# Three causal heads in a bank of sums instead of two, in a four-layer transformer kernel on one Trainium2 core

## The chip, the cores and the metric

One core of one Trainium2 chip runs the whole program in one launch. The metric is device time in microseconds (us) for one execution. The kernel before took 1213.9 us as the median of 3 runs (1211.96 to 1216.73).

## The reference

Two sequences of 1024 tokens, width 128, pass through four residual layers, each followed by a layer norm: causal attention with 16 heads of 8, a mixture of 8 experts (top 2 of 8, ReLU), a second causal attention with 16 heads of 8 whose queries and keys are low-rank products, and a last layer that is an attention without a mask (16 heads, 4 values a head) followed by a mixture of 8 experts with GELU. What this case touches is the end of each head's attention:

```python
attn = softmax(where(causal, scale * q @ k.T, -inf))   # per head, 1024 x 1024
ans  = attn @ v                                        # per head, 1024 x 8
x    = layernorm(x + ans_of_all_heads @ Wo.T + bo)
```

All arithmetic that the reference does in float32 is kept to float32 accuracy: queries and keys are split into three bf16 parts, and the product with the values is a float32 matmul.

## The kernel before

Engines run five instruction streams that are written out by hand and meet only at semaphores. There are 96 heads in all, numbered g: 0 to 31 are the first causal attention (16 heads for each of two sequences), 32 to 63 the second, 64 to 95 the attention without a mask. Run 0 is heads 0 to 31, then come 32 units of the first experts; run 1 is heads 32 to 95, then the second experts.

A causal head has 9 chunks of 512 columns in two batches (k=0 has five, k=1 four). For each chunk TensorE (PE) computes a block of scores by query (L1246), whose row maxima VectorE (DVE) takes two heads ahead (L974, L980), and a block of scores by key (L1261), which ScalarE (ACT) turns into probabilities (L864). Three banks (S1, S2) stand between PE and each of its two readers. `probs_by_v` then multiplies the probabilities of a batch by the values: 18 matmuls a head, in the order: batch 1 of the head before in this head's k=0, batch 0 of this head in its k=1. The maxima come back to PE through GpSimd (POOL, `split_max`, L673 to L680), one transpose on PE (`max_rows`, L1269), ACT (`rows`, L841) and a DMA.

The product with the values leaves its sums, transposed, in one bank, SUM. Its left operand is a head's tile of 32 columns in `v_heads`: POOL (`take_v`, L656) copies the head's 9 columns (a one for the denominator and 8 values) to the place of the head in its group and the other columns stay zero. So several heads can add into SUM side by side: a group. A causal group is two heads (2 x 9 = 18 of 32 columns), a group without mask four heads. There are four such value tiles, by g modulo 4.

When a group has ended, SUM has to be emptied:

- ACT `take_sums` (L846) copies the bank, PE waits for that before the first product of the next group
- PE `turn_sums` (L1296) turns it with 4 float32 transposes into the bank SHARED, at k=1 of the next head
- ACT `take_out` (L848) copies the used columns to `by_quarter`
- POOL `add_quarters` (L683) adds up the four quarters with 3 instructions, before its second mask and `split_max` of the same head
- DVE `normalise` (L990) takes a reciprocal and multiplies, in the middle of the head after that.

SHARED is used by nearly everything else too: `max_rows` of each head, and the steps of the surrounding layers (output projections, layer norms' transposes, routing, the next layer's queries, keys and values), which a table puts between the batches of given heads (L259 to L299). Each user of SHARED waits until the one before has been read out (`move_in`). The table's steps stand at the same heads before and after; the steps `aT` (turning the attention's output) wait for all groups of a sequence.

Of the kernel before, what the change touches and what calls it, by code (L numbers as in the profile page):

```python
# [1 line left out]

# [39 lines left out]
class Attention:  # L42


    def __init__(self, layer, head_dim, scale_dim, causal):
# [4 lines left out]
        self.dv = head_dim + 1  # L50
        self.group = 16 // head_dim
        self.scale = float(scale_dim) ** -0.5
# [39 lines left out]
class Head:  # L92


    def __init__(self, g):
# [4 lines left out]
        self.slot = g % RING  # L100
        self.first_of_group = self.n % self.a.group == 0
        self.ends_group = self.n % self.a.group == self.a.group - 1

# [28 lines left out]
GROUP = [sum(hd.ends_group for hd in HEADS[:g]) for g in range(3 * NH + 1)]  # L132
GROUPS = [[hd for hd in HEADS if GROUP[hd.g] == i] for i in range(GROUP[-1])]
ADDS = [sum(heads[0].a.adds for heads in GROUPS[:i]) for i in range(len(GROUPS) + 1)]

# [182 lines left out]
def build(nc, inp, out):  # L318
    ctx = ExitStack()
    with ctx:  # L320
        def sb(name, shape, dt=F32):
            return ctx.enter_context(nc.sbuf_tensor(name, shape, dt))
# [19 lines left out]
        v_all = [sb("v8", [P, NH, TB, 9]), sb("v4", [P, NH, TB, 5])]  # L342
        v_heads = [sb("v_head8", [P, RING, TB, Q]), sb("v_head4", [P, RING, TB, Q])]
        probs = sb("probs", [P, 9, CH])
        sums = sb("sums", [P, 2, CH])
        by_quarter = sb("by_quarter", [P, 2, 4, 4, 20])
        pairs = sb("pairs", [P, 4, 18])
        total = sb("total", [P, 2, TB, 20])
        tile_max = sb("tile_max", [P, RING, TB, 3])
# [45 lines left out]
        def v_head_of(a):  # L395
            return v_heads[0 if a.hd == 8 else 1]
# [179 lines left out]
        def _(pool):  # L576
# [79 lines left out]
            def take_v(g):  # L656
                hd = HEADS[g]
                a = hd.a
                ge(pool, "pv", BATCHES[max(g - RING + 1, 0)])
                if a.layer == 0 and hd.n == 0:  # L660
                    pool.wait_ge(sem("v_first"), NCH)
                if a.layer > 0 and hd.h == 0:
                    taken(pool, "v", a.layer, BY_SEQUENCE[hd.b][-1])
                at = a.dv * (hd.n % a.group)
                nc.gpsimd.tensor_copy(v_head_of(a)[:, hd.slot, :, at:at + a.dv], v_of(a)[:, hd.n, :, :]
                                      ).then_inc(sem("v_head"), 1)
# [16 lines left out]
            def add_quarters(i):  # L683

                a = GROUPS[i][0].a
                q = by_quarter[:, i % 2, :, :, 0:a.group * a.dv]
                pool.wait_ge(sem("by_quarter"), i + 1)
                ge(pool, "normalised", 2 * (i - 1))
                if not a.causal:
                    nc.gpsimd.tensor_tensor(  # L690
                        total[:, i % 2, :, 0:a.group * a.dv].rearrange("p (half t) d -> p t half d", half=2),
                        q[:, :, 0:4:2, :], q[:, :, 1:4:2, :], ALU.add).then_inc(sem("total"), 1)
                    return
                ge(pool, "total", ADDS[i])
                nc.gpsimd.tensor_tensor(pairs[:], q[:, :, 0, :], q[:, :, 1, :], ALU.add).then_inc(sem("total"), 1)  # L695
                pool.wait_ge(sem("total"), ADDS[i] + 1)
                nc.gpsimd.tensor_tensor(total[:, i % 2, 4:8, 0:18], pairs[:], q[:, :, 2, :], ALU.add
                                        ).then_inc(sem("total"), 1)
                nc.gpsimd.tensor_copy(total[:, i % 2, 0:4, 0:18], q[:, :, 3, :]).then_inc(sem("total"), 1)

# [41 lines left out]
        def _(act):  # L742
# [105 lines left out]
            def take_out(i):  # L848
                a = GROUPS[i][0].a
                act.wait_ge(sem("out"), i + 1)  # L850
                ge(act, "total", ADDS[max(i - 1, 0)])
                nc.scalar.activation(by_quarter[:, i % 2, :, :, 0:a.group * a.dv],  # L852
                                     SHARED[:].rearrange("p (t g c) -> p t g c", t=4, g=4)[:, :, :, 0:a.group * a.dv],
                                     ACT.Copy).then_inc(sem("by_quarter"), 1)
# [54 lines left out]
        def _(dve):  # L909
# [80 lines left out]
            def normalise(i):  # L990
                first = GROUPS[i][0]
                a, G, h = first.a, first.a.group, first.h
                o = total[:, i % 2, :, 0:G * a.dv].rearrange("p t (g d) -> p t g d", g=G)
# [177 lines left out]
        def _(pe):  # L1171
# [100 lines left out]
            def probs_by_v(g, k):  # L1272
# [10 lines left out]
                for c, b in a.pv_order[k]:  # L1283
                    if c in a.masked and (c, b) == next(y for y in a.pv_order[k] if y[0] == c):
# [4 lines left out]
                    this = (c, b, half, quarter)  # L1289
                    ins = mm(SUM[Q * quarter:Q * (quarter + 1), q:q + P * count], v_head_of(a)[:, hd.slot, j, :],  # L1290
                             probs[:, hd.probs_place(c), at:at + P * count],
# [11 lines left out]
            def between(place):  # L1303
                for step in BETWEEN[place]:
# [3 lines left out]
                    if kind == "aT":  # L1308
                        L, c = which
                        a = ATTENTIONS[L]  # L1310
                        groups_done = (L * NH + H * (c // CB + 1)) // a.group if L < 2 else (
                            GROUP[2 * NH] + H * (c // CB + 1) // a.group)
                        pe.wait_ge(sem("normalised"), 2 * groups_done)
# [208 lines left out]
```

## Time and profile before

| | |
|---|---|
| median of 3 runs | 1213.9 us |
| the profiled execution | 1214.44 us, of which its span 1212.7 us, granted PE clock 0.985 |
| PE busy | 1108.5 us (91%) |
| DVE busy | 870.5 us (72%) |
| ACT busy | 777.6 us (64%) |
| POOL busy | 270.3 us (22%) |

Busy time says which engine works, and not which one the others wait for. In the causal heads the program is periodic, so the time between two equal instructions of neighbouring heads says directly what a head costs. The instruction used for that is `rows` (L841 on ACT), once a head, at the end of its first batch.

### The profile page before, as it was taken

What the parts mean: (1) busy time and instruction counts of PE and PEld (TensorE: products, weight loads), DVE (VectorE), ACT (ScalarE), POOL (GpSimd) and SP (SyncE); (2) the same over time, 40 slices, a digit from 0 to 9 for tenths busy, and PEclk for the clock granted to TensorE, in tenths of its full rate; (3) what the DMA queues carried; (4) which work ended last, traced back from release to release, by engine and by line L of the source; (5) the groups of instructions that cost most, each with busy time, mean ns of one, the idle gap of its engine ahead of it and who ended that gap; (6) DMA issues with size and microseconds to landing.
All of it is one profiled execution on the core that took longest, in us unless ns stands there. A gap on an engine that the chain in (4) does not pass through costs nothing. (4 is left out here: it accounts for less than half of the span.)

```text
span 1212.7 us, 24956 instructions
## 1 busy us (share of the span) xinstructions
PE 1108.5 (91%) x8799; PEld 605.9 (50%) x8872; DVE 870.5 (72%) x2077; ACT 777.6 (64%) x1563; POOL 270.3 (22%) x819
## 2 busy tenths in 40 slices
PE   8899998999999988999988998888888898899996
PEld 6466665656766655666655642221112221137774
DVE  4888887773434377888766899899999889904433
ACT  4376766667444436777666667888888778874443
POOL 4244332332002013533233421111110011000001
PEclk9899999999999999999999999999999989999999
DMA  7245431110001701243211321102111000000000
GB/s 192 57 111 135 113 93 32 40 32 2 1 1 23 165 11 41 74 104 95 71 48 58 62 39 33 29 12 35 37 33 29 20 12 16 7 1 1 10 9 18
DMA packets 39550, 57.67 MB, mean 48 GB/s; under 512 B 9393, under 2 KB 14977, under 8 KB 39041
## 3 DMA queue, kind: packets, MB, share of 16 engines
q1 hardware_dynamic: 39424, 56.06, 18.7%
q8 instruction: 71, 1.16, 0.4%
q14 instruction: 55, 0.44, 0.1%
HBM read 30.81 MB, written 24.64 MB: 46 GB/s over the span
## 5 line engine op out<-in xcount | busy, mean ns | idle before, releaser
L864 ACT ACTIVATE probs<-bank 128x512 f32<-128x512 f32 x1088 | 574.6, 601 | 235.2 <-PE bank L1261 234.2
L980 DVE TENSOR_REDUCE tile_max<-bank 128x1 f32<-128x512 f32 (+3 forms) x1152 | 612.3, 593 | 38.0 <-PE bank L1246 33.3
L1246 PE MATMUL bank<-qk 125*128 125x128 bf16 (+2 forms) x1664 | 389.0, 312 | 59.1 <-DVE tile_max L980 46.7
L1261 PE MATMUL bank<-qk 128*128 128x128 bf16 (+4 forms) x1607 | 362.8, 306 | 5.7 <-ACT probs L864 5.3
L1290 PE MATMUL bank<-probs,v_head 128*32 128x512 f32 (+3 forms) x3328 | 304.3, 454 | 0.1
L1246 PEld LDWEIGHTS bank<-qk 125*128 125x128 bf16 (+1 forms) x1664 | 132.2, 97 | 316.9 <-DVE tile_max L980 244.2
L1147 DVE SCALAR_TENSOR_TENSOR acc<-bank,gate,acc 128x128 f32<-128x128 f32 x256 | 72.0, 344 | 156.7 <-PE bank L1417 156.7
L1290 PEld LDWEIGHTS bank<-probs,v_head 128*32 128x32 f32 x3328 | 139.7, 109 | 52.8 <-issue 29.8
L1261 PEld LDWEIGHTS bank<-qk 128*128 128x128 bf16 (+1 forms) x1664 | 133.2, 97 | 56.8 <-ACT probs L864 21.0
L884 ACT ACTIVATE probs<-bank,sb_b 128x512 f32<-128x512 f32 x128 | 81.0, 684 | 117.9 <-PE bank L1406 117.9
L974 DVE TENSOR_REDUCE tile_max<-bank 128x4 f32<-128x512 f32 x128 | 87.4, 688 | 87.0 <-PE bank L1246 86.7
L1417 PEld LDWEIGHTS bank<-sb_w,probs 128*128 128x128 f32 x1024 | 123.1, 192 | 24.5 <-issue 24.0
L1417 PE MATMUL bank<-sb_w,probs 128*128 128x128 f32 x1024 | 124.7, 275 | 0.0
L1406 PE MATMUL bank<-xT,sb_w 128*128 128x512 f32 x256 | 121.0, 595 | 0.0
L705 POOL TENSOR_SCALAR_AFFINE_SELECT probs<-probs 128x512 f32<-128x512 f32 x128 | 81.6, 638 | 133.6 <-ACT probs L864 133.4
L673 POOL CAST neg_parts<-neg_max 128x8 bf16<-128x8 f32 x96 | 18.5, 193 | 325.9 <-DVE neg_max L987 325.9
L1406 PEld LDWEIGHTS bank<-xT,sb_w 128*128 128x128 f32 x256 | 43.9, 191 | 34.1 <-issue 33.8
L695 POOL TENSOR_TENSOR pairs<-by_quarter 128x72 f32<-128x72 f32 x32 | 11.0, 344 | 159.3 <-ACT by_quarter L852 159.3
L1241 PE MATMUL bank<-mask,ident 128*128 128x512 bf16 x112 | 43.7, 391 | 2.6 <-DVE tile_max L980 1.2
L841 ACT ACTIVATE neg_rows<-bank 24x128 bf16<-24x128 bf16 x96 | 24.7, 257 | 20.2 <-PE bank L1269 20.2
L641 POOL TENSOR_SCALAR rstd<-mean_var 128x4 f32<-128x4 f32 (+1 forms) x12 | 2.9, 238 | 146.0 <-DVE mean_var L1038 145.7
L804 ACT ACTIVATE x<-x_plus,shift,rstd 128x128 f32<-128x128 f32 x64 | 26.2, 487 | 9.8 <-POOL shift L644 9.8
(133 smaller groups left out, 659.8 us busy)
## 6 DMA issues: line engine op xcount, KB each, us to landing
qk<-qk_parts SPq DMA_DIRECT2D x160, 144.0 KB
qk_parts<-q_parts SPq DMA_DIRECT2D x48, 192.0 KB, 2.4
qk_parts<-k_parts SPq DMA_DIRECT2D x48, 192.0 KB, 3.0
qk_parts<-q_parts SPq DMA_DIRECT2D x24, 96.0 KB, 2.3
qk_parts<-k_parts SPq DMA_DIRECT2D x24, 96.0 KB, 2.9
sb_w<-in_w SPq DMA_DIRECT2D x8, 256.0 KB, 3.8
sb_w<-in_w SPq DMA_DIRECT2D x2, 1024.0 KB, 5.6
qk<-neg_rows SPq DMA_DIRECT2D x96, 6.0 KB
```

The costliest lines, as they stand in the source:

```text
L705: nc.gpsimd.affine_select(out=p, in_=p, compare_op=ALU.is_ge, fill=0.0, base=0, pattern=[[0, 4], [1, P]], channel_multiplier=-1).then_inc( ...
L864: nc.scalar.activation(probs[:, hd.probs_place(c), :], S2[i % len(S2)][:], ACT.Exp, scale=hd.a.scale).then_inc(sem("probs"), 1)
L884: nc.scalar.activation(hidden[:, m % 2, fb, :], bank[2 * (m % 2) + fb][:], ACT.Relu if f == 0 else ACT.Gelu, bias=w_sb[f"b1_{f}"][:, FB * ...
L974: ins = nc.vector.tensor_reduce(tile_max[:, hd.slot, 4 * c:4 * c + 4, 0], s1[:].rearrange("p (t k) -> p t k", k=P), AX.X, ALU.max)
L980: ins = nc.vector.tensor_reduce(tile_max[:, hd.slot, t, which:which + 1], s1[:, at:at + P * count], AX.X, ALU.max)
L1147: ins = nc.vector.scalar_tensor_tensor(acc[:, tile, :], Y[m % 2][:, P * t:P * (t + 1)], gate[:, tile, e:e + 1], acc[:, tile, :], ALU.mult, ...
L1241: mm(s1[:], ident16[:], mask16[:].rearrange("p t k -> p (t k)"), start=True, stop=False, skip_group_check=True)
L1246: ins = mm(s1[:, at:at + P * count], qk[hd.query_rows, hd.place, 0, P * t:P * (t + 1)], qk[hd.query_rows, hd.place, 1, P * k0:P * (k0 + co ...
L1261: ins = mm(s2[:, at:at + P * count], qk[hd.key_rows, hd.place, 1, P * j:P * (j + 1)], qk[hd.key_rows, hd.place, 0, P * q0:P * (q0 + count) ...
L1290: ins = mm(SUM[Q * quarter:Q * (quarter + 1), q:q + P * count], v_head_of(a)[:, hd.slot, j, :], probs[:, hd.probs_place(c), at:at + P * co ...
L1406: ins = mm(bank[2 * (m % 2) + fb][:], w_sb[f"w1_{f}"][:, e, P * fb:P * (fb + 1)], xT[:, tokens(c)], start=True, stop=True)
L1417: ins = mm(Y[m % 2][:, P * t:P * (t + 1)], hidden[:, m % 2, fb, P * t:P * (t + 1)], w_sb[f"w2_{f}"][:, e, fb, :], start=fb == 0, stop=fb = ...
```

## The change

The 16 causal heads of a sequence are grouped 3, 3, 3, 3, 2, 2 where they were grouped in eight pairs. A group of three uses 27 of the 32 columns. Because a value tile's zero columns must stay zero, a tile now belongs to a place in the group: six tiles, three places for each of two alternating groups, and `take_v` waits for the head that used the same tile last. The evacuation of a group, its three adds and its normalisation work on 27 columns a tile where the group has three heads, and on 18 where it has two. The attention without a mask keeps its groups of four.

```diff
-        self.group = 16 // head_dim
+        self.groups = (3, 3, 3, 3, 2, 2) if causal else (4, 4, 4, 4)
...
-        self.first_of_group = self.n % self.a.group == 0
-        self.ends_group = self.n % self.a.group == self.a.group - 1
+        ends = list(accumulate(self.a.groups))
+        group = sum(self.h >= end for end in ends)
+        self.at_in_group = self.h - ends[group] + self.a.groups[group]
+        self.first_of_group = self.at_in_group == 0
+        self.ends_group = self.h == ends[group] - 1
+        self.v_slot = self.at_in_group + 3 * (group % 2) if self.a.causal else self.slot
...
+V_BEFORE = {hd.g: max((o.g for o in HEADS[:hd.g] if o.a.causal == hd.a.causal and o.v_slot == hd.v_slot), default=None)
+            for hd in HEADS}
...
-        v_heads = [sb("v_head8", [P, RING, TB, Q]), sb("v_head4", [P, RING, TB, Q])]
+        v_heads = [sb("v_head8", [P, 6, TB, Q]), sb("v_head4", [P, RING, TB, Q])]
-        by_quarter = sb("by_quarter", [P, 2, 4, 4, 20])
-        pairs = sb("pairs", [P, 4, 18])
-        total = sb("total", [P, 2, TB, 20])
+        by_quarter = sb("by_quarter", [P, 2, 4, 4, 27])
+        pairs = sb("pairs", [P, 4, 27])
+        total = sb("total", [P, 2, TB, 27])
...
-                ge(pool, "pv", BATCHES[max(g - RING + 1, 0)])
+                if V_BEFORE[g] is not None:
+                    pool.wait_ge(sem("pv"), BATCHES[V_BEFORE[g] + 1])
...
-                at = a.dv * (hd.n % a.group)
-                nc.gpsimd.tensor_copy(v_head_of(a)[:, hd.slot, :, at:at + a.dv], v_of(a)[:, hd.n, :, :]
+                at = a.dv * hd.at_in_group
+                nc.gpsimd.tensor_copy(v_head_of(a)[:, hd.v_slot, :, at:at + a.dv], v_of(a)[:, hd.n, :, :]
...
-                nc.gpsimd.tensor_tensor(pairs[:], q[:, :, 0, :], q[:, :, 1, :], ALU.add).then_inc(sem("total"), 1)
+                nc.gpsimd.tensor_tensor(pairs[:, :, 0:wide], q[:, :, 0, :], q[:, :, 1, :], ALU.add).then_inc(sem("total"), 1)
...
-                a = GROUPS[i][0].a
+                wide = GROUPS[i][0].a.dv * len(GROUPS[i])
...
-                a, G, h = first.a, first.a.group, first.h
+                a, G, h = first.a, len(GROUPS[i]), first.h
...
-                        groups_done = (L * NH + H * (c // CB + 1)) // a.group if L < 2 else (
-                            GROUP[2 * NH] + H * (c // CB + 1) // a.group)
+                        groups_done = GROUP[L * NH + H * (c // CB + 1)]
```

How the streams change is seen at two places. The first is PE in head 34, the third of the second causal attention, from the last scores of its batch 1 to the product with the values and the projection behind it. Before (L1261 scores by key, L1300 the turn of the sums, L1290 the product with the values, L1369 a projection of the table):

```order
L1261 MATMUL bank<-qk 128x384 [waits probs]
L1261 MATMUL bank<-qk 128x128
L1300 MATMUL bank<-ident,sums 128x128 [waits taken,sums]
L1300 MATMUL bank<-ident,sums 128x128 x3
L1290 MATMUL bank<-probs,v_head 32x512 [waits probs,sums,v_head]
L1290 MATMUL bank<-probs,v_head 32x512 x2
L1290 MATMUL bank<-probs,v_head 32x256
L1290 MATMUL bank<-probs,v_head 32x128 [waits masked]
L1290 MATMUL bank<-probs,v_head 32x256
L1290 MATMUL bank<-probs,v_head 32x128 x3
L1369 MATMUL bank<-xT,wk_eff 128x512 [waits by_quarter,taken,loaded_attn1]
```

The same place in the changed kernel (its lines are 10 or 11 higher):

```order
L1272 MATMUL bank<-qk 128x384 [waits probs]
L1272 MATMUL bank<-qk 128x128
L1301 MATMUL bank<-probs,v_head 32x512 [waits probs,v_head]
L1301 MATMUL bank<-probs,v_head 32x512 x2
L1301 MATMUL bank<-probs,v_head 32x256
L1301 MATMUL bank<-probs,v_head 32x128 [waits masked]
L1301 MATMUL bank<-probs,v_head 32x256
L1301 MATMUL bank<-probs,v_head 32x128 x3
L1379 MATMUL bank<-xT,wk_eff 128x512 [waits taken,loaded_attn1]
```

The turn of the sums, with its wait for SHARED (`taken`) and for `sums`, has left head 34; it stands in head 35 now.

The second place is POOL in head 52, from the copy of a value tile (L665) to the splitting of the next maxima (L673). Before:

```order
L665 COPY v_head<-v 128x8x9 [waits pv]
L695 TENSOR_TENSOR pairs<-by_quarter 128x72 [waits total,normalised,by_quarter]
L697 TENSOR_TENSOR total<-pairs,by_quarter 128x4x18 [waits total]
L699 COPY total<-by_quarter 128x4x18
L705 AFFINE_SELECT probs<-probs 128x512 [waits probs]
L641 TENSOR_SCALAR rstd<-mean_var 128x8 [waits var]
L642 TENSOR_TENSOR rstd<-rstd,minus_half 128x8 [waits gpsimd_chain]
L643 TENSOR_TENSOR shift<-mean_var,rstd 128x8 [waits gpsimd_chain]
L644 TENSOR_SCALAR shift<-shift 128x8 [waits gpsimd_chain]
L673 CAST neg_parts<-neg_max 128x8 [waits neg_max,neg_ps]
```

In the changed kernel:

```order
L675 COPY v_head<-v 128x8x9 [waits pv]
L716 AFFINE_SELECT probs<-probs 128x512 [waits probs]
L650 TENSOR_SCALAR rstd<-mean_var 128x8 [waits var]
L651 TENSOR_TENSOR rstd<-rstd,minus_half 128x8 [waits gpsimd_chain]
L652 TENSOR_TENSOR shift<-mean_var,rstd 128x8 [waits gpsimd_chain]
L653 TENSOR_SCALAR shift<-shift 128x8 [waits gpsimd_chain]
L683 CAST neg_parts<-neg_max 128x8 [waits neg_max,neg_ps]
```

The three adds of the sums, which wait for ACT's `by_quarter`, are gone from between the copy and the mask; they stand in head 51, as 128x108.

## Rows read from the trace of the kernel before

**Rows 1.** Timeline of ACT: start us, duration us, engine, line, operation (heads 1 to 4).
```profile
54.95 0.26 ACT L841 ACTIVATE neg_rows<-bank 24x128 bf16<-24x128 bf16 x1
...
62.03 0.26 ACT L841 ACTIVATE neg_rows<-bank 24x128 bf16<-24x128 bf16 x1
...
69.56 0.26 ACT L841 ACTIVATE neg_rows<-bank 24x128 bf16<-24x128 bf16 x1
...
76.86 0.26 ACT L841 ACTIVATE neg_rows<-bank 24x128 bf16<-24x128 bf16 x1
```
**Rows 2.** Timeline of PE in head 40, the turn and what follows.
```profile
519.62 0.60 PE L1300 MATMUL bank<-ident,sums 128*128 128x128 f32 x4
520.15 1.51 PE L1290 MATMUL bank<-probs,v_head 128*32 128x512 f32 x18
```
**Rows 3.** Timeline of DVE (the multiply of `normalise`, heads 41 and 5) and POOL (head 5).
```profile
525.00 0.29 DVE L997 TENSOR_TENSOR a_tok<-total,den_inv 128x128 f32<-128x128 f32 x1
...
84.51 0.48 DVE L997 TENSOR_TENSOR a_tok<-total,den_inv 128x128 f32<-128x128 f32 x1
...
83.55 1.29 POOL L631 TENSOR_TENSOR x_plus<-x,sb_bo 128x512 f32<-128x512 f32 x1
```
**Rows 4.** Groups by shape: busy us, mean ns of one.
```profile
L995 DVE RECIPROCAL den_inv<-total 128x16 f32<-128x16 f32 x32 | 7.8, 245 | 7.3 <-POOL total L699 7.3
...
L995 DVE RECIPROCAL den_inv<-total 128x32 f32<-128x32 f32 x8 | 2.7, 344 | 0.0
...
L1027 DVE TENSOR_TENSOR x_plus<-x,acc 128x512 f32<-128x512 f32 x4 | 2.9, 718 | 0.0
...
L695 POOL TENSOR_TENSOR pairs<-by_quarter 128x72 f32<-128x72 f32 x32 | 11.0, 344 | 159.3 <-ACT by_quarter L852 159.3
...
L690 POOL TENSOR_TENSOR total<-by_quarter 128x160 f32<-128x160 f32 x8 | 4.2, 522 | 56.1 <-ACT by_quarter L852 56.1
...
L852 ACT ACTIVATE by_quarter<-bank 128x288 f32<-128x288 f32 x32 | 13.5, 422 | 1.3 <-PE bank L1300 1.2
```
**Rows 5.** Timeline of POOL, end of `split_max`, and of PE, its reader, head 41.
```profile
523.09 0.20 POOL L680 TENSOR_TENSOR neg_parts<-neg_rest,neg_parts 128x8 bf16<-128x8 f32 x1
...
524.14 0.23 PE L1269 MATMUL bank<-ident,neg_parts 128*24 128x128 bf16 x1
```
**Rows 6.** Timeline of PE, turns in heads 34, 56 and 18.
```profile
472.20 0.63 PE L1300 MATMUL bank<-ident,sums 128*128 128x128 f32 x4 [0.94 <-DVE rest L937]
...
659.75 0.63 PE L1300 MATMUL bank<-ident,sums 128*128 128x128 f32 x4 [1.06 <-DVE rest L938]
...
185.68 0.63 PE L1300 MATMUL bank<-ident,sums 128*128 128x128 f32 x4 [0.22 <-ACT aT L794]
```
**Rows 7.** Timeline of ACT, heads 52 and 21.
```profile
612.33 0.25 ACT L841 ACTIVATE neg_rows<-bank 24x128 bf16<-24x128 bf16 x1
...
623.20 0.25 ACT L841 ACTIVATE neg_rows<-bank 24x128 bf16<-24x128 bf16 x1
...
210.13 0.26 ACT L841 ACTIVATE neg_rows<-bank 24x128 bf16<-24x128 bf16 x1
...
218.96 0.25 ACT L841 ACTIVATE neg_rows<-bank 24x128 bf16<-24x128 bf16 x1
```
**Rows 8.** Timeline of PE around the start of head 53.
```profile
621.33 0.23 PE L1269 MATMUL bank<-ident,neg_parts 128*24 128x128 bf16 x1 [2.01 <-POOL neg_parts L680]
...
623.59 1.08 PE L1338 MATMUL bank<-ident,x 128*128 128x128 f32 x4 [1.17 <-ACT neg_rows L841]
```
**Rows 9.** Busy time by stretch; the third number from the end is the granted PE clock.
```profile
622.00:625.00 3.00, 1.83 (x17) 1.25 (x11) 0.00 (x0) 1.45 (x4) 0.07 (x1) 0.67 0.01 2
625.00:628.00 3.00, 2.78 (x26) 1.77 (x27) 2.67 (x6) 2.18 (x5) 0.83 (x2) 0.76 0.05 8
```
**Rows 10.** Timeline of POOL at the start of the program.
```profile
7.59 1.90 POOL L608 MEMSET v_head<- 128x1024 f32 x2
...
14.43 2.28 POOL L618 TENSOR_TENSOR k_parts<-rest,k_parts 128x512 bf16<-128x512 f32 x2 [4.57 <-ACT k_parts L754]
```

More of the change, by code:

```diff
@@ L1 @@
 from contextlib import ExitStack
+from itertools import accumulate
 import concourse.bass as bass
@@ L685, in add_quarters @@
                 a = GROUPS[i][0].a
-                q = by_quarter[:, i % 2, :, :, 0:a.group * a.dv]
+                wide = a.dv * len(GROUPS[i])
+                q = by_quarter[:, i % 2, :, :, 0:wide]
                 pool.wait_ge(sem("by_quarter"), i + 1)
@@ L690, in add_quarters @@
                     nc.gpsimd.tensor_tensor(
-                        total[:, i % 2, :, 0:a.group * a.dv].rearrange("p (half t) d -> p t half d", half=2),
+                        total[:, i % 2, :, 0:wide].rearrange("p (half t) d -> p t half d", half=2),
                         q[:, :, 0:4:2, :], q[:, :, 1:4:2, :], ALU.add).then_inc(sem("total"), 1)
@@ L694, in add_quarters @@
                 ge(pool, "total", ADDS[i])
-                nc.gpsimd.tensor_tensor(pairs[:], q[:, :, 0, :], q[:, :, 1, :], ALU.add).then_inc(sem("total"), 1)
+                nc.gpsimd.tensor_tensor(pairs[:, :, 0:wide], q[:, :, 0, :], q[:, :, 1, :], ALU.add).then_inc(sem("total"), 1)
                 pool.wait_ge(sem("total"), ADDS[i] + 1)
-                nc.gpsimd.tensor_tensor(total[:, i % 2, 4:8, 0:18], pairs[:], q[:, :, 2, :], ALU.add
+                nc.gpsimd.tensor_tensor(total[:, i % 2, 4:8, 0:wide], pairs[:, :, 0:wide], q[:, :, 2, :], ALU.add
                                         ).then_inc(sem("total"), 1)
-                nc.gpsimd.tensor_copy(total[:, i % 2, 0:4, 0:18], q[:, :, 3, :]).then_inc(sem("total"), 1)
+                nc.gpsimd.tensor_copy(total[:, i % 2, 0:4, 0:wide], q[:, :, 3, :]).then_inc(sem("total"), 1)
             def mask(g, which):
@@ L848, in take_out @@
             def take_out(i):
-                a = GROUPS[i][0].a
+                wide = GROUPS[i][0].a.dv * len(GROUPS[i])
                 act.wait_ge(sem("out"), i + 1)
                 ge(act, "total", ADDS[max(i - 1, 0)])
-                nc.scalar.activation(by_quarter[:, i % 2, :, :, 0:a.group * a.dv],
-                                     SHARED[:].rearrange("p (t g c) -> p t g c", t=4, g=4)[:, :, :, 0:a.group * a.dv],
+                nc.scalar.activation(by_quarter[:, i % 2, :, :, 0:wide],
+                                     SHARED[:].rearrange("p (t g c) -> p t g c", t=4, g=4)[:, :, :, 0:wide],
                                      ACT.Copy).then_inc(sem("by_quarter"), 1)
@@ L1289, in probs_by_v @@
                     this = (c, b, half, quarter)
-                    ins = mm(SUM[Q * quarter:Q * (quarter + 1), q:q + P * count], v_head_of(a)[:, hd.slot, j, :],
+                    ins = mm(SUM[Q * quarter:Q * (quarter + 1), q:q + P * count], v_head_of(a)[:, hd.v_slot, j, :],
                              probs[:, hd.probs_place(c), at:at + P * count],
```

## The prediction

> **What bounds the kernel now.** I read the timeline of ACT first, for the time from one `rows` to the next in the causal heads. A head is one of three kinds. In a turn head the group of the head before is evacuated (PE's four transposes); in a normalise head, the one after it, DVE does the two instructions of `normalise`; in a plain head neither happens. The kernel before has turn and normalise heads in strict alternation, with one plain head in the clear, head 1, before any group has ended. Plain 62.03 - 54.95 = 7.08 us, turn 69.56 - 62.03 = 7.53, normalise 76.86 - 69.56 = 7.30 [rows 1]. The same 7.53 and 7.30 come back in the quiet heads of both layers. So a group boundary costs 0.45 + 0.22 us over two plain heads, whatever the engines' busy shares say.
>
> Next the timeline of PE says what the 0.45 is: PE has no idle in a turn head, and from the turn's first transpose to the product behind it is 520.15 - 519.62 = 0.53 us [rows 2]. PE ends that head. In the normalise head DVE's work in the middle makes PE wait for a bank of maxima. How directly it does so is seen where POOL works beside it: in head 5 a 1.29 us POOL addition of a bias started at 83.55, and the multiply at 84.51 took 0.48 instead of 0.29 [rows 3]; that head's period is longer by about the same 0.19. Time added to `normalise` comes through one for one.
>
> Last come the heads in which a turn meets a step of the table, since the change moves turns: PE's own waits before L1300 [rows 6] and the costliest wait at a max transpose [rows 8].
>
> **The change part by part.**
>
> Groups. A sequence had 8 turn and 8 normalise heads; with turns behind heads 2, 5, 8, 11, 13 and 15 it has 6 turn, 6 normalise and 4 plain heads. Over four sequences 8 turns go at 0.45 = -3.6 us and 8 normalisations at 0.22 = -1.8 us [rows 1]. ACT's and POOL's share of a boundary (copying the bank, evacuating 288 columns at 0.42, the adds) lies beside PE's work and is counted as nothing. What is late next in a plain head is what is late in head 1: PE's own matmuls and DVE's maxima, both near 7.0.
>
> Biases. The four POOL bias additions of layer 0 run in heads 5, 7, 9, 11, and one of layer 1 in head 37, all normalise heads before. Of these only head 7 is one afterwards. 4 x 0.19 = -0.8 us [rows 3]. Bounds: 0 (they disturb something else) to -0.9. The Trainium skill, "SBUF — State Buffer", in its terms on the shared port pair, says that VectorE and GpSimd hold it exclusively for a whole instruction and the loser is fully blocked. By that rule each multiply would wait for the end of the bias addition, 84.84 - 84.51 = 0.33, and the sum would be 0.6 lower; the row shows 0.19, so the trace agrees only in direction.
>
> Wider work. 16 groups have 27 columns a tile where 18 were. On DVE: the reciprocal goes from 16 to 24 elements, halfway between 245 and 344 ns, +0.05; the multiply gets 64 more elements, at (718 - 292)/384 = 1.1 ns (292 is the 128-element multiply, 0.29 in the rows) +0.07 [rows 3, 4]. 16 x 0.12 = +1.9 us, all exposed as argued. Bounds: 0, and in proportion to the columns, half of 0.245 + 0.29, so 16 x 0.27 = +4.3. I take 1.9, as it has a slope from rows. On ACT and POOL: the evacuation 0.42 becomes at most 0.63; the two-input adds cost (522 - 344)/88 = 2.0 ns an element, so 344 becomes 417 [rows 4], the three together +0.2. `split_max` is queued behind them on POOL, and PE's max transpose waits for it: `split_max` ends 523.29, the transpose starts 524.14, so 0.85 us are free [rows 5]. Even in proportion (+0.46 for the adds, +0.21 on ACT) it fits. Cost nothing.
>
> Value tiles. `take_v` waits for a product that is 4 to 6 heads old, or older, instead of 4: never later than before. The value tile's clearing at the start grows from 1024 to 1536 elements, half of 1.90/2 = +0.5 us on POOL (at most +0.95), which then waits 4.57 us for ACT anyway [rows 10]. Nothing.
>
> Turns that leave a collision. Before, PE in heads 34 and 56 reached the turn while SHARED still held queries of the next layer, not yet read out: it waited 0.94 and 1.06 us [rows 6]. Both become plain heads. The product behind does not use SHARED, and the next user comes behind it, 1.5 us later [rows 2], so the wait goes: -2.0. Heads 18 and 50 waited 0.22 each for `aT` and become plain: -0.4 [rows 6]. In exchange turns come to heads 19, 25, 35, 51 and 57. Only in 35 (values of the next layer) and 51 (a projection) does SHARED have a tenant from the same head; both are read out by DVE at about the time PE arrives. Bounds 0 to 2 x 1.06; I take +0.3, an estimate: a readout by one quick instruction, as the 0.22 us wait for `aT`, in each or less. Together -2.1 us.
>
> Head 52. Here POOL had the three adds, the mask and the root of the layer norm ahead of `split_max`, and PE stood 2.01 us at the max transpose, then 1.17 for SHARED [rows 8]. The period was 623.20 - 612.33 = 10.87. Head 21 has the same steps of the other layer in a normalise head, without adds: 218.96 - 210.13 = 8.83 [rows 7]. In the changed kernel head 52 is a normalise head. 10.87 - 8.83 = 2.04, of which 7.53 - 7.30 = 0.23 is already counted: -1.8 us. After these waits PE's granted clock was 0.67 and 0.76 over two stretches of 3 us, that is 1.2 GHz instead of 2.4 for 2 x 0.33 x 3 = 2.0 and 2 x 0.24 x 3 = 1.4 us [rows 9]. If PE no longer stands so long, the matmuls in 3.4 us run in half the time: up to -1.7; bounds 0 and -1.7, I take half, -0.9, since another wait for SHARED remains there.
>
> Sum: -3.6 - 1.8 - 0.8 + 1.9 - 2.1 - 1.8 - 0.9 = -9.1 us. Against the profiled execution's 1214.44 (span 1212.7 and 1.7 around it) that is 1205.3. The median of the runs is 0.5 lower than that execution, less than their spread, so I leave 1205.3. All else, experts and attention without mask, is taken as unchanged.
>
> **The rivals.**
>
> A. The collisions only move. The table is dense in heads 17 to 28 and 49 to 56, and a turn in 19, 25, 35 or 51 or a wider normalisation in 52 can meet what the old ones met. For it: three of the old turns waited on exactly such steps. Against: head 21 shows the combination of head 52 without harm. Then only the regular part is left: -3.6 - 1.8 - 0.8 + 1.9 = -4.3, so 1210.1.
>
> B. A plain head in the steady state is no better than a normalise head, because head 1 stands next to the start and nothing else shows the kind; DVE is then the next limit. Turns give 8 x 0.23 = -1.8, normalisations 0, the rest as summed (-0.8 + 1.9 - 2.1 - 1.8 - 0.9): -5.5, so 1208.9; with A too, 1213.7. Against: a turn head has no idle on PE, so without the turn 7.53 - 0.53 = 7.00 us of PE's work are left [rows 1, 2], which is near head 1.
>
> C. More comes off: the wider normalisation is hidden (0 instead of +1.9) and the whole 1.7 of clock comes back: -11.8, so 1202.6.
>
> D. Slower: POOL's chain from the evacuation over the wider adds to `split_max` gets so long that PE waits at the max transpose in each of the 16 wide turn heads, as it did in head 52. It bites from 0.85 us of growth [rows 5]. Growth of 1.4 eats the whole gain (16 x 0.57 = 9.1). At 1.9, adds some three times as long, 16 x 1.05 = 16.8, so 1205.3 + 16.8 = 1222.1. Against: the rows' slopes give 0.3 and proportion 0.67.
>
> **How the numbers follow.** Forecast 0.53, own range 1202.5 to 1208; A 0.20; B 0.12 (a third of it with A); C 0.09; D 0.06. What a measurement can tell from no change is about 0.5%, 6.1 us: faster means below 1207.8. Forecast 0.50 and C 0.09, little of B 0.04 and of A 0.03: faster 0.66. Same: most of A and B and a rest of the forecast, 0.28. D makes slower 0.06. The range 1200.5 to 1211.5 takes in C with some clock beyond it, A and most of B, and is open to D and to B with A.
>
> **What would show it.** In the quiet heads of each layer `rows` should come at 7.53, 7.42, 7.08 in turn; 7.3 for the third means B. `normalise` should be about 0.30 and 0.36 us long. PE should have no wait before the turn over 0.3 us, else A. The 2.01 us wait before the max transpose of head 53 should be gone, and the clock dip with it or halved. POOL's `pairs` addition should take 0.42 us; a growing count of PE waits for `neg_parts` means D. I am wrong if the experts or heads from 65 on change by more than a microsecond.

## The result, and the profile after

The changed kernel took 1208.9 us (median of 6 runs, 1207.54 to 1212.2) against 1213.5 for the kernel before on the same chip (6 runs, 1211.96 to 1216.73): ratio 0.9958, 95% interval 0.9945 to 0.9972, 4.6 us or 0.4% less. The forecast was 9.1 us less, and 1208.9 lies 0.9 above its own range (1202.5 to 1208), inside the wide one (1200.5 to 1211.5). The 0.4% is below the 0.5% from which on the prediction spoke of faster, so by this measurement its likeliest outcome did not come. A second measurement of the same kernel (first experiment) gave 0.9935 (0.992 to 0.9951), 7.3 less, with 17 runs of before beside it. The profiled execution of the first, 1212.2 us (span 1210.5, granted clock 0.982), is the slowest of its six. So the lines in this section are from its profile, but the sums by head further down are made from the second's, 1207.9 (span 1206.2, clock 0.986). From profile to profile the heads agree to 0.01 or 0.02 us, except where the clock fell.

PE is busy 1106.1 us (91%), DVE 868.8, ACT 772.7, POOL 268.1: each engine within 5 us of before, which doesn't say where the difference lies.

The first view is ACT's timeline in heads 1 to 4, which answers to [rows 1] (the lines are 11 higher).

```profile
55.92 0.26 ACT L852 ACTIVATE neg_rows<-bank 24x128 bf16<-24x128 bf16 x1
...
63.00 0.26 ACT L852 ACTIVATE neg_rows<-bank 24x128 bf16<-24x128 bf16 x1
...
70.09 0.26 ACT L852 ACTIVATE neg_rows<-bank 24x128 bf16<-24x128 bf16 x1
...
77.62 0.26 ACT L852 ACTIVATE neg_rows<-bank 24x128 bf16<-24x128 bf16 x1
```

Heads 1 and 2 are plain, 7.08 and 7.09, and head 3 is the turn, 7.53. The quiet heads repeat 7.53, 7.41, 7.08.

The wider operations, by shape (busy us, mean ns of one), beside [rows 3, 4]:

```profile
L1008 DVE TENSOR_TENSOR a_tok<-total,den_inv 128x192 f32<-128x192 f32 x16 | 6.8, 425 | 0.5
L706 POOL TENSOR_TENSOR pairs<-by_quarter 128x108 f32<-128x108 f32 x16 | 6.7, 419 | 80.1 <-ACT by_quarter L863 80.1
L1006 DVE RECIPROCAL den_inv<-total 128x24 f32<-128x24 f32 x16 | 4.7, 292 | 0.0
```

The reciprocal's 292 (forecast 295) and the add's 419 (417) are as read from the slopes, and ACT's evacuation takes 0.535 us (at most 0.63 was allowed for). The multiply's mean, 425, is above the 0.36 us that it takes alone: two of the 16 are long. They belong to what was missed. This is DVE and POOL in head 36 and then in head 7:

```profile
487.56 1.01 DVE L1008 TENSOR_TENSOR a_tok<-total,den_inv 128x192 f32<-128x192 f32 x1
...
487.19 1.16 POOL L627 TENSOR_TENSOR q_parts<-rest,q_parts 128x512 bf16<-128x512 f32 x1
...
99.80 0.79 DVE L1008 TENSOR_TENSOR a_tok<-total,den_inv 128x192 f32<-128x192 f32 x1
...
99.09 1.28 POOL L640 TENSOR_TENSOR x_plus<-x,sb_bo 128x512 f32<-128x512 f32 x1
```

And in head 57, now a turn head, PE waits for POOL. The timelines of PE and POOL there:

```profile
662.86 0.61 PE L1311 MATMUL bank<-ident,sums 128*128 128x128 f32 x4
...
669.29 0.23 PE L1280 MATMUL bank<-ident,neg_parts 128*24 128x128 bf16 x1 [1.84 <-POOL neg_parts L690]
```

```profile
664.17 0.42 POOL L706 TENSOR_TENSOR pairs<-by_quarter 128x108 f32<-128x108 f32 x1 [5.00 <-ACT by_quarter L863]
...
665.23 0.64 POOL L716 TENSOR_SCALAR_AFFINE_SELECT probs<-probs 128x512 f32<-128x512 f32 x1
665.83 1.15 POOL L627 TENSOR_TENSOR q_parts<-rest,q_parts 64x512 bf16<-64x512 f32 x1
666.95 1.15 POOL L627 TENSOR_TENSOR k_parts<-rest,k_parts 64x512 bf16<-64x512 f32 x1
668.05 0.18 POOL L683 CAST neg_parts<-neg_max 128x8 bf16<-128x8 f32 x1
...
669.04 0.20 POOL L690 TENSOR_TENSOR neg_parts<-neg_rest,neg_parts 128x8 bf16<-128x8 f32 x1
```

The turn itself waits for nothing. But behind the three adds (the first is shown) and the mask POOL has two instructions of a step of the table. They split off the third bf16 part of queries and keys for the layer without mask (the "thirds" from here on), 2.3 us together, and `split_max` comes behind them. The last two of these four rows of ACT show what it costs: 8.96 us for head 57 (660.59 to 669.55), where the normalise head before took 7.30.

```profile
611.15 0.25 ACT L852 ACTIVATE neg_rows<-bank 24x128 bf16<-24x128 bf16 x1
620.24 0.25 ACT L852 ACTIVATE neg_rows<-bank 24x128 bf16<-24x128 bf16 x1
...
660.59 0.25 ACT L852 ACTIVATE neg_rows<-bank 24x128 bf16<-24x128 bf16 x1
669.55 0.27 ACT L852 ACTIVATE neg_rows<-bank 24x128 bf16<-24x128 bf16 x1 [1.28 <-PE bank L1280]
```

The first two rows are head 52: 9.09, where [rows 7] gave 10.87. PE's max transpose at its end waits for nothing (it waited 2.01 [rows 8]); the wait for SHARED behind it is still there, 1.59 us where it was 1.17:

```profile
620.63 0.63 PE L1348 MATMUL bank<-ident,x 128*128 128x128 f32 x4 [1.59 <-ACT neg_rows L852]
```

After it PE's clock is at full in the stretches of [rows 9]:

```profile
622.00:625.00 3.00, 2.80 (x34) 2.18 (x33) 1.23 (x4) 2.67 (x7) 0.79 (x4) 1.00 0.31 98
625.00:628.00 3.00, 2.91 (x32) 1.65 (x29) 3.00 (x7) 2.89 (x7) 0.83 (x2) 1.00 0.00 0
```

### The profile page after: what moved, and what is told of

It reads as the page before. It is cut to its first block and busy times, and to the rows that moved or that the text cites. A ratio compares the mean times of both kernels' runs of the same rounds, so it can differ in the third digit from the quotient of the medians.

```text
span 1210.5 us, 24804 instructions
## 1 busy us (share of the span) xinstructions
PE 1106.1 (91%) x8768; PEld 605.3 (50%) x8840; DVE 868.8 (72%) x2061; ACT 772.7 (64%) x1547; POOL 268.1 (22%) x795
## 5 line engine op out<-in xcount | busy, mean ns | idle before, releaser
L706 POOL TENSOR_TENSOR pairs<-by_quarter 128x108 f32<-128x108 f32 (+1 forms) x24 | 9.5, 395 | 122.5 <-ACT by_quarter L863 122.5
```

## The experiments

Each edit is to the changed kernel, except where it says otherwise.

### The same kernel again, and groups of two in the new tiles

`a_again` has no edit. `two_by_place` keeps the tiles by place and everything else, with pairs in them:

```diff
-        self.groups = (3, 3, 3, 3, 2, 2) if causal else (4, 4, 4, 4)
+        self.groups = (2, 2, 2, 2, 2, 2, 2, 2) if causal else (4, 4, 4, 4)
```

> The changed kernel again, unaltered, to see which differences from the kernel before come back. Theory 1 (a fixed cost per kind of head plus meetings of turns with steps of the table): the same periods to 0.02 us in the quiet heads (7.53, 7.41, 7.08), 8.96 in head 57 and 8.06 in head 36, while the extra 1.6 us of head 23 and the 2.9 us of heads 61 to 63, where the granted PE clock fell, are not tied to the change and need not come back; ratio to before 0.9955 to 0.9965. Theory 2 (the moved turns bring the clock down at heads 23 and 61 to 63): both dips come back at the same heads with the same cost.

> One part of the change alone: six value tiles by place, evacuation and adds with a width by group, but groups of two heads everywhere. Theory 1 (all of the effect is in the number of groups): turn 7.53 and normalise 7.30 in every pair of heads, ratio to before 0.999 to 1.001. Rival (take_v's later wait or the larger clearing at the start counts): the start of head 0 moves by 0.5 us or more, ratio off by 0.002 or more.

Measured on one chip: 1207.9 us (0.9935) for the changed kernel again, and 1215.5 (12 runs) with pairs, ratio 1.0005 (0.9993 to 1.0017).

In `a_again` the quiet heads and heads 57 and 36 come back as expected. Of the falls of the clock, the one in head 23 came back (11.17) and those in heads 61 to 63 did not, so each theory was right about one of them.

With pairs the heads' periods add up to 0.24 us over before. Its first `rows` comes at 41.19 us, 0.9 later than before, which the rival asked for, but the changed kernel itself has it at 41.11 in one profile and 39.92 in the other, so a single start says nothing. The tiles, their larger clearing and `take_v`'s wait cost nothing that these runs can show; the gain is the grouping's.

### The steps that the new heads met, moved

The table counts in batches, half a head each. POOL's thirds for queries and keys come three batches after their step by default; `thirds_later` puts the last at five, one head later (58, a normalise head now). `all_moved` also moves the thirds of head 36 by half a head, and the bias addition of head 7 by one head.

```diff
-place = put_qkv(2, 1, later(place, 3))
+place = put_qkv(2, 1, later(place, 3), (0, 1, 2, 5))
```

```diff
-for c, g in enumerate((4, 6, 8, 10)):
+for c, g in enumerate((4, 7, 8, 10)):
...
-def put_next_qkv(c, place):
+def put_next_qkv(c, place, offsets=range(4)):
...
-    return put_qkv(1, c, later(place, 1))
+    return put_qkv(1, c, later(place, 1), offsets)
...
-put_next_qkv(3, at_head(32, 0))
+put_next_qkv(3, at_head(32, 0), (0, 1, 2, 4))
```

> The changed kernel with the step `third` of head 57 moved to head 58 (and the stores that follow it one head later). Theory 1 (in head 57 POOL has three wider adds, the mask and two thirds of 1.15 us ahead of split_max, and PE waits 1.84 us for it): head 57 falls from 8.96 to 7.53, the 1.84 us wait before the max transpose goes, head 58 stays within 0.3 of 7.57, in sum -1.3 to -1.7 us against the changed kernel. Rival (the wait only moves to head 58, or the time is given back in heads 61 to 63, where DVE is the bound): heads 57 to 64 together lose less than 0.4 us.

> The same, and two more moves of steps away from normalise heads: the bias addition of head 7 to head 8, the thirds of head 36 half a head later. Theory 1 (POOL's two-input instructions hold up the wide multiply of normalise on DVE: it took 1.01 us in head 36 instead of 0.36): head 36 falls from 8.06 to 7.45, head 7 from 7.84 to 7.41, in sum -2.3 to -2.8 us against the changed kernel, ratio to before 0.9935 to 0.9945. Rival (the long multiply is not on the path of PE): the multiply gets short and the periods stay.

`thirds_later` took 1205.5 us (1204.9 to 1207.6), 0.9921 (0.9907 to 0.9936), 2.4 below the unaltered kernel on the same chip. Its heads 57 and 58 together are 1.6 shorter, which the theory had at 1.3 to 1.7; the rest is not explained by the move. Heads 57 and 58 in ACT's timeline, and PE's max transpose in the former, which has no wait now:

```profile
658.91 0.25 ACT L852 ACTIVATE neg_rows<-bank 24x128 bf16<-24x128 bf16 x1
666.44 0.26 ACT L852 ACTIVATE neg_rows<-bank 24x128 bf16<-24x128 bf16 x1
673.86 0.26 ACT L852 ACTIVATE neg_rows<-bank 24x128 bf16<-24x128 bf16 x1
...
665.70 0.23 PE L1280 MATMUL bank<-ident,neg_parts 128*24 128x128 bf16 x1
```

7.53 and 7.42, the quiet values. So the 1.4 us that head 57 took over a quiet turn head is the meeting of the adds with the thirds in one POOL queue. In `all_moved` the multiply of head 36 is alone and takes 0.36:

```profile
487.14 0.36 DVE L1008 TENSOR_TENSOR a_tok<-total,den_inv 128x192 f32<-128x192 f32 x1
```

Head 36 takes 7.42 instead of 8.06, and head 7 7.42 instead of 7.84: the heads show the 1.1 us. The time does not: 1206.2 us, 0.9919 (0.9904 to 0.9934), no different from `thirds_later`, and 1.7 below the unaltered kernel where 2.3 to 2.8 was expected. In its profile the clock fell in head 23, as in the unaltered kernel.

### The same collision made in the kernel before

`before_thirds` is the kernel before with the last thirds moved from its head 57 (normalise there) to head 58 (a turn there), the edit of `thirds_later`.

> The kernel before, groups of two, with the thirds of head 57 moved to head 58, which is a turn head in it. Theory 1 (adds, mask and thirds in one turn head make POOL late for split_max): the mirror image of what happened in head 57 of the changed kernel, a wait of PE for POOL of 1.3 to 1.9 us in head 58 and a period of about 9 instead of 7.53, total +1.3 to +1.8 us, ratio 1.001 to 1.0015. Rival (the wait in head 57 came from the wider adds and not from the meeting): head 58 stays under 7.9.

ACT's and PE's timeline in that head:

```profile
673.99 0.26 ACT L841 ACTIVATE neg_rows<-bank 24x128 bf16<-24x128 bf16 x1
682.58 0.27 ACT L841 ACTIVATE neg_rows<-bank 24x128 bf16<-24x128 bf16 x1 [0.90 <-PE bank L1269]
...
682.31 0.23 PE L1269 MATMUL bank<-ident,neg_parts 128*24 128x128 bf16 x1 [1.46 <-POOL neg_parts L680]
```

8.59 us where it took 7.53, +1.1 (about 9 was expected), and PE waits 1.46 for the same tile; head 59 behind it takes 7.56 instead of 7.30. The mechanism belongs to a turn head whose adds and thirds both stand ahead of `split_max` in POOL's queue, whatever the width of the groups. It is the order that matters: in the kernel before, thirds also ran at head 36, a turn head, but they had ended 2.1 us before its adds, and the head took the quiet 7.53. That the wider adds deepen the wait fits its 1.84 us against 1.46, in two different heads. The whole time, 1216.5 us in 10 runs, 1.0009 (0.999 to 1.0028), is too coarse for it.

### Each part of a boundary doubled

`turn_twice` turns the sums twice, `multiply_twice` does the multiply of `normalise` once more beforehand into an unused tile, `pairs_twice` the first of POOL's adds.

```diff
-                for t in range(4):
+                for t in [0, 1, 2, 3] * 2:
```

```diff
+                nc.vector.tensor_tensor(
+                    spare[:, i % 2, :, 0:G * a.hd].rearrange("p t (g d) -> p t g d", g=G),
+                    o[:, :, :, 1:a.dv], den_inv[:, i % 2, :, 0:G].unsqueeze(3).to_broadcast([P, TB, G, a.hd]),
+                    ALU.mult)
```

```diff
+                nc.gpsimd.tensor_tensor(spare[:, i % 2, :, 0:wide], q[:, :, 0, :], q[:, :, 1, :], ALU.add)
```

> The changed kernel with the four transposes of each turn of the sums done twice into the same places (32 turns, 30 of them in heads). Theory (PE alone ends a turn head): each of the 22 causal turn heads gets longer by 0.53 us, 7.53 becomes 8.06, while the turn heads of the attention without mask, where DVE is busier, grow by less; in sum +11 to +17 us. Rival (the turn head is set by ACT or DVE and the transposes lie in a gap): under +5 us.

> The changed kernel with normalise's multiply done once more into an unused tile before the real one. Theory (DVE's time in normalise comes through to PE one for one): wide normalise heads go from 7.41 to about 7.7 and those of two heads from 7.29 to about 7.5. Rival (part is hidden): the quiet normalise heads grow by less than 0.15 us.

> The changed kernel with POOL's first add of the quarters done once more into an unused tile, +0.42 us ahead of split_max in each wide turn head. Theory (0.85 us were free in quiet turn heads, a little over 0.5 are left): quiet turn heads stay 7.53, head 57, where PE already waits for POOL, grows by 0.4. Rival D of the prediction (POOL's chain is at the edge): quiet turn heads grow by 0.2 us or more.

`turn_twice`, ACT around its turn head 3 and the doubled turn on PE:

```profile
68.32 0.26 ACT L852 ACTIVATE neg_rows<-bank 24x128 bf16<-24x128 bf16 x1
76.28 0.26 ACT L852 ACTIVATE neg_rows<-bank 24x128 bf16<-24x128 bf16 x1
...
70.59 1.04 PE L1311 MATMUL bank<-ident,sums 128*128 128x128 f32 x8
```

7.96 for 7.53: a second turn costs 0.43, as the first does (7.53 - 7.09 = 0.44). The theory had 0.53, the distance in [rows 2] from the first transpose to the product; 0.1 of it isn't added by the turn. The turn heads without mask grow by the same (head 72 from 11.03 to 11.47), not by less. There are 24 turns of causal groups and 8 of the others, 32 x 0.43 = 13.8; measured 1220.6 us, 1.0055 (1.0037 to 1.0073), that is 6.4 above before where the unaltered kernel is 7.3 below: 13.7. So close an agreement has luck in it: the medians are from two chips, and the two profiles' spans differ by 15.7, with falls of the clock in different heads.

`multiply_twice` (a single run, 1214.6 us), ACT around its wide normalise head 4:

```profile
76.80 0.27 ACT L853 ACTIVATE neg_rows<-bank 24x128 bf16<-24x128 bf16 x1
84.48 0.27 ACT L853 ACTIVATE neg_rows<-bank 24x128 bf16<-24x128 bf16 x1
```

7.68 for 7.41, +0.27 for an instruction whose row says 0.36. But 0.36 isn't what it takes from DVE. Here are the added multiply and the real one behind it, DVE in the same head:

```profile
76.97 0.36 DVE L1009 TENSOR_TENSOR spare<-total,den_inv 128x192 f32<-128x192 f32 x1
77.24 0.35 DVE L1013 TENSOR_TENSOR a_tok<-total,den_inv 128x192 f32<-128x192 f32 x1
```

They start 0.27 apart: the row's duration overlaps the next instruction by 0.09. With groups of two the starts are 0.20 apart, and those heads grow by 0.20 (7.29 to 7.49). So time added to `normalise` comes through one for one, as the theory and the prediction had it, if it is read from start to start. The forecast's 0.12 for the wider work holds too. From the start of the reciprocal to the next maximum DVE takes 0.60 us in a wide head and 0.49 in a narrow one, and the heads take 7.41 and 7.30. Of the 0.49 a narrow normalise head shows 0.21 over a plain one, so the first 0.28 is hidden, and what comes on top is not.

In head 36 the same edit costs 1.21 us, from 8.06 to 9.27. DVE and POOL there:

```profile
486.83 0.99 DVE L1009 TENSOR_TENSOR spare<-total,den_inv 128x192 f32<-128x192 f32 x1
487.75 1.30 DVE L1013 TENSOR_TENSOR a_tok<-total,den_inv 128x192 f32<-128x192 f32 x1
...
486.45 1.16 POOL L628 TENSOR_TENSOR q_parts<-rest,q_parts 128x512 bf16<-128x512 f32 x1
487.56 1.27 POOL L628 TENSOR_TENSOR k_parts<-rest,k_parts 128x512 bf16<-128x512 f32 x1
```

Each multiply runs into a POOL instruction of its own and ends 0.21 and 0.22 us after it (487.82 against 487.61, 489.05 against 488.83).

`pairs_twice` (a single run, 1212.3 us), ACT in the quiet turn head 41, then PE in head 57:

```profile
524.89 0.26 ACT L854 ACTIVATE neg_rows<-bank 24x128 bf16<-24x128 bf16 x1
532.42 0.26 ACT L854 ACTIVATE neg_rows<-bank 24x128 bf16<-24x128 bf16 x1
...
669.93 0.23 PE L1282 MATMUL bank<-ident,neg_parts 128*24 128x128 bf16 x1 [2.15 <-POOL neg_parts L691]
```

In a quiet turn head 0.4 more on POOL costs nothing (7.53). In head 57 the wait grows from 1.84 to 2.15, by 0.3 where 0.4 was expected. So the room that the prediction read from [rows 5] is there, and used up where POOL has a step. The delay shows in two normalise heads as well: in heads 7 and 36 POOL's long instruction starts later, the multiply beside it takes 1.13 and 1.37 us instead of 0.79 and 1.01, and the heads grow by the same 0.34 and 0.36.

### A head in which the clock fell

Head 23 took 9.57 us before and 11.17 after. It is a normalise head in both, and wider work can't be 1.6 us. In both, the step that turns `x` waits 2.01 us for SHARED, until ACT's `rows` has read the maxima out. Behind that wait the clock fell in the profile of after and not in that of before. The stretch that follows it, before and after, busy time and granted clock (third number from the end):

```profile
230.00:234.00 4.00, 4.00 (x42) 3.10 (x40) 2.22 (x6) 2.27 (x5) 1.42 (x5) 1.00 0.22 74
```

```profile
230.00:234.00 4.00, 4.00 (x35) 2.69 (x33) 1.27 (x3) 1.45 (x3) 0.79 (x4) 0.75 0.22 74
```

`xt_later` moves the step that waits (turning `x`) one head on, out of the way of that wait; `moved_xt` has it and the three other moves.

```diff
-put_routing(0, 0, put_attention_out(0, 0, at_head(17, 1), (0, 1, 2, 4, 5, 7, 8, 10, 11, 12)),
+put_routing(0, 0, put_attention_out(0, 0, at_head(17, 1), (0, 1, 2, 4, 5, 7, 8, 10, 12, 13)),
```

> The changed kernel with the second transposing step `xT` of the first attention moved from the middle of head 23 to its end, and the routing steps behind it half a head later. Theory 1 (in head 23 PE stands 2.01 us for SHARED because ACT does a layer norm before it reads out the maxima; the granted clock then falls or not depending on how that wait lies, 11.17 with the fall and 9.57 without): without the wait PE goes on, the clock stays at 2.4 GHz through head 23, and heads 22 to 29 together lose 2.5 to 4 us against the changed kernel. Theory 2 (the fall of the clock comes from the moved turn at head 22 or 25 and not from the wait): head 23 keeps a stretch with a granted clock of 0.5 to 0.7 and a period over 10.5.

> All moves together: thirds of head 57, bias of head 7, thirds of head 36 and the second xT of the first attention. Theory 1: the parts add up, ratio to before 0.988 to 0.991. Rival (the routing steps, half a head later, meet the turns of heads 25 and 28 or the end of the run and give it back): 0.9915 or more.

ACT's `rows` of `xt_later` in heads 22 to 24, and the moved transposes:

```profile
227.32 0.25 ACT L852 ACTIVATE neg_rows<-bank 24x128 bf16<-24x128 bf16 x1
234.17 0.27 ACT L852 ACTIVATE neg_rows<-bank 24x128 bf16<-24x128 bf16 x1
245.00 0.25 ACT L852 ACTIVATE neg_rows<-bank 24x128 bf16<-24x128 bf16 x1
...
229.93 0.66 PE L1348 MATMUL bank<-ident,x 128*128 128x128 f32 x4
...
243.85 0.39 PE L1257 MATMUL bank<-qk 125*128 125x256 bf16 x2 [1.83 <-DVE tile_max L991]
```

Its stretch behind the transposes:

```profile
230.00:234.00 4.00, 4.00 (x44) 2.71 (x43) 2.93 (x7) 2.71 (x6) 0.83 (x2) 1.00 0.17 62
```

The wait of 2.01 is gone, the clock stays at full, and head 23 takes 6.85. But head 24 takes 10.83 where it took 7.98, with 1.83 us of waiting for DVE's maxima: the work came along. Heads 22 to 29 together took 2.04 less than in the profile of after, where 2.5 to 4 was expected, and of that 1.6 is the clock fall that it had and this one had not. Nor does the full clock in head 23 tell the theories apart, since the kernels with the step in its old place have it in some profiles too (below). The time, 1208.5 us, 0.9943 (0.9925 to 0.9962), is that of the unaltered kernel. A miss. `moved_xt` took 1205.1 us, 0.9917 (0.9899 to 0.9934), again that of `thirds_later`: the parts did not add up in the time, and the rival's 0.9915 or more is what came.

Last, `all_moved` and `moved_xt` were measured again, as `all_moved_2` and `moved_xt_2`, since 6 runs each could not tell them apart.

> The version with the three moves of POOL steps again, beside the version with all four moves on the same chip. Theory 1: its heads 23 and 57 have 11.17 and 7.53 as before; it is 1 to 3 us slower than the version with all moves. Rival (what xT later saves is lost to the clock elsewhere): the two are within 0.5 us.

> The version with all four moves again. Theory 1: heads 23 and 24 have 6.85 and 10.83, the clock stays up in 23; 1 to 3 us faster than the version with three moves, ratio to before 0.990 to 0.992.

`all_moved_2` took 1205.6 us, 0.9924 (0.9901 to 0.9948), and `moved_xt_2` 1204.6, 0.9903 (0.9878 to 0.9929). Their intervals overlap, and they stay together. What they do settle is something about head 23. Here are PE's transposes in `all_moved` and the granted clock over the stretch behind them, and then both in `all_moved_2`, which is the same program:

```profile
227.08 0.63 PE L1348 MATMUL bank<-ident,x 128*128 128x128 f32 x4 [2.01 <-ACT neg_rows L852]
```

```profile
230.00:234.00 4.00, 4.00 (x37) 3.02 (x35) 0.91 (x3) 1.09 (x3) 0.79 (x4) 0.80 0.22 74
```

```profile
225.84 0.63 PE L1348 MATMUL bank<-ident,x 128*128 128x128 f32 x4 [2.01 <-ACT neg_rows L852]
```

```profile
226.00:230.00 4.00, 4.00 (x42) 2.77 (x41) 2.73 (x6) 2.56 (x5) 1.38 (x5) 1.00 0.12 24
```

The same program with the same wait: in one execution the clock falls and the head takes 11.17, in the other it stays at full and the head takes 9.57, where the expectation had 11.17. So neither the change nor the wait decides it alone. Whether the change makes the fall likelier is not shown: of the eight profiles with groups of three and this step in place five have it, of the three with groups of two none. `moved_xt_2`'s profile had falls elsewhere, in heads 24 and 25 (12.47 and 9.38 us, where `moved_xt` took 10.83 and 7.77).

## Why the prediction was partly right

The direction and most of the mechanism held. The forecast time was 3.6 us too low by the first measurement, and the forecast gain 1.8 us too large by the second. The table puts the differences of the heads' periods, before to `a_again`, to the prediction's steps. Its first row is what a quiet head's change of kind measures (8 turns at 0.44, 8 normalisations at 0.21, 16 wider ones at 0.11), applied to all 64 causal heads; the others are what a head differs beyond that. The 35 causal heads that are in no other row agree with it within 0.02 us each.

| step | forecast | measured |
|---|---|---|
| turns and normalisations fewer, wider work | -3.5 | -3.4 |
| biases | -0.8 | -0.6 |
| heads 34, 56 | -2.0 | -2.4 |
| heads 18, 50 | -0.4 | -0.8 |
| new turns in 19, 25, 35, 51 | +0.3 | -0.1 (35 alone +0.3) |
| head 52 | -1.8 | -1.7 |
| clock after head 52 (head 53) | -0.9 | -1.0 |
| **sum of what was forecast** | **-9.1** | **-9.9** (rows unrounded) |
| head 57: adds and thirds in POOL's queue | 0 | +1.4 |
| head 36: wide multiply beside thirds | 0 | +0.6 |
| heads 21, 24, 27 gain less than a plain head should (+0.7), smaller differences (-0.2) | 0 | +0.5 |
| clock: head 23, start of run 1, head 84 | 0 | +1.5, +0.6, -1.1 |
| **all heads** | **-9.1** | **-6.4** |

**Groups.** 0.44 for a turn and 0.21 or 0.22 for a normalisation, as read from four rows of ACT; `turn_twice` shows the first by itself, and `multiply_twice` that work added to `normalise` is exposed one for one. Rival B (a plain head no better) is refuted: quiet plain heads take 7.08 in both layers.

**Biases.** Heads 5, 9, 11 and 37 gave 0.17 to 0.19 each beyond their kind, and head 10 0.13. Head 7 was said to keep its addition beside a multiply, and does, but that multiply was 0.47 before and is 0.79 now: 0.24 more than the wider work accounts for. The prediction had put the cost of such a meeting at what one row showed (0.19), though what a meeting costs depends on how much of POOL's instruction is left; the last section works that out.

**Head 52 and the clock.** Both terms held within 0.2 (-1.7 and -1.0 for -1.8 and -0.9). The root of the layer norm now stands in a POOL queue without adds, PE's max transpose of head 53 waits for nothing, and the clock is at full in the two windows in which it was 0.67 and 0.76 [rows 9]. This fall is tied to the grouping: all three profiles with groups of two have it there and none of the eleven with groups of three. That -0.9 came near is partly luck: it was half of an upper bound, for a clock that would come back in part. The clock came back whole, and the longer wait for SHARED (1.59 us for 1.17) took some of it away. Head 21 as the stand-in for head 52 was a good choice.

**Turns that leave a collision: the step that failed.** The prediction weighed new turn heads by one question only, who holds SHARED. That part came out better than forecast (34, 56, 18, 50, and 51). But a turn head also brings three adds to POOL, and a normalise head a multiply to DVE, and both meet POOL's other steps. The table's thirds (L627) stand in heads 36 and 57, and neither was read. Rival A said that collisions would move, in heads 19, 25, 35, 51 or 52. Only 35 shows any (+0.3, as much as was allowed for all four); the costly ones moved to 57 and 36. Rival D had the right place, POOL's chain to `split_max` with 0.85 us of room, and looked for the growth in the adds' width. There it is 0.3, as forecast; it is in head 57 that something else of 2.3 us stands in the same queue. `thirds_later` gives back what this cost in head 57 and `before_thirds` makes the same in the kernel before. With head 57 quiet, the kernel gained 9.7 us by the medians of its runs; that this is near the forecast's 9.1 is partly luck, since heads 57 and 58 account for 1.6 of the 2.4 between the two medians.

**A plain head in the dense stretch.** Head 24 was to gain 0.45 as a plain head and gained nothing. DVE is the limit there: in the 8 us of the head it is busy 7.78 us in both kernels, as it also does the routing's top 2 there (L1054 to L1077 in the changed kernel), while PE's busy time fell from 7.95 to 7.64. Heads 21 and 27 gained 0.07 and 0.11 where 0.21 was due; what ends them is not shown. That the price of an operation in a quiet head doesn't apply there was not weighed.

**Clock.** Apart from head 53, clock falls in head 23, at the start of run 1 and in head 84 (which had its fall before) added 1.0 in this profile, and more in the profile of the first measurement (heads 61 to 63 +2.9). In head 84 the granted clock is 0.71 over 5 us in the profile of before and 1.00 in that of `a_again`, with not one instruction of the change in it, and `pairs_twice` has the 13.48 us of before again, while `before_thirds`, with groups of two, takes 12.42. So the heads from 65 on did change by 1.1 us, which the prediction had named as a sign of being wrong; it is this fall alone. Such falls come and go between executions, as head 23 shows for one program; they are within the spread of the runs, 2.7 to 9 us.

What stays open: which condition makes the clock fall in head 23, whether the change makes that likelier, and whether `all_moved` or `moved_xt` is the better by anything. The five measurements with the last thirds moved lie at 1204.6 to 1206.2 us, 0.9903 to 0.9924 of before, and their intervals overlap. Lowest of all is `moved_xt`; the simplest that does as well within what can be measured is `thirds_later`, one number in the table.

## What to carry to other kernels

When a change moves work from one period of a pipeline to another, list for each receiving period what every engine of the moved chain already has in its queue there, not only who holds the buffer that the first link wants: the turn was free, and its adds two engines on were not. The price of an operation is read in quiet periods, and it is the price only there; in a crowded period it is nothing or several times as much. Where two engines' instructions can start in each other's way, take the whole length of the longer one as the upper bound, for each instruction that can meet one. And what an instruction adds to its engine is read from start to start, not from its duration.

## What the hardware showed that was not expected

A multiply of two inputs on DVE takes 0.36 us alone and 1.01 in head 36, beside a POOL addition. It started 0.37 us after the latter (487.56 against 487.19) and ended at 488.57, 0.22 after POOL's end at 488.35. In head 7 it ended at 100.59, 0.22 after POOL's end at 100.37. The five further meetings in these heads of `multiply_twice` and `pairs_twice` give 0.21 or 0.22 again, with multiplies of 0.78 to 1.37 us. That is no slowing in proportion: DVE's instruction ends at one distance from the end of POOL's, whenever it began. The Trainium skill, "SBUF — State Buffer", in its terms on the shared port pair, has the loser fully blocked for the instruction of the other; the trace agrees, and more clearly than in the row that the prediction used, where the 0.48 us multiply ended 0.15 after POOL [rows 3].

That row fits the others, though the prediction read it as agreeing only in direction. In all three the multiply got longer by what was left of POOL's instruction when it started, less 0.14 us: 0.33 left and 0.19 longer in head 5, 0.57 and 0.43 in head 7, 0.79 and 0.65 in head 36. Heads 7 and 36 grew by the same 0.43 and 0.65 over the quiet 7.41. So the price of a meeting is not one number, and goes up to nearly the length of the other engine's instruction.

One program, with one wait of 2.01 us before PE's transposes in head 23, ran on at 2.4 GHz in one execution and had a mean granted clock of 0.80 over 4 us in another, part of it at 1.2 GHz, at a cost of 1.6 us (9.57 and 11.17).
